# A decoder kernel: the clearing of a sorted buffer is issued later in SP's queue, from other zeros

## The reference

```python
x = x + attention(layernorm(x))          # linear attention, 16 heads, elu(q), elu(k), silu(v), gate silu(u)
x = x + experts(layernorm(x), token_ids) # 4 experts, each with one 512 x 512 matrix ctx[e] as gate, up and down
x = x + ffn(x)                           # W_up, W_gate, W_down of 2048 x 512, made ternary by their mean |w|
```

## Time and profile before

| | us |
|---|---|
| median of 3 runs | 761.21 (761.17 to 762.01) |
| the profiled execution, its own time | 762.63 |
| its span, first to last instruction | 761.0 |
| TensorE busy | 714.1 (94% of the span) |
| VectorE busy | 388.2 |
| ScalarE busy | 276.2 |
| GpSimd busy | 108.1 |
| mean granted clock of TensorE | 0.978 of full speed |

### The profile page before, as it was taken

The page is one execution under the profiler, slowest core; times in us unless marked ns, Lnnn a source line. Parts: engine busy times, 40 slices in busy tenths (PEclk is TensorE's granted clock), DMA queues, the critical chain, the costliest instruction groups (busy, mean ns, idle before and its releaser), DMA issues.

```text
span 761.0 us, 11666 instructions
## 1 busy us (share of the span) xinstructions
PE 714.1 (94%) x3804; PEld 378.2 (50%) x3835; DVE 388.2 (51%) x672; ACT 276.2 (36%) x430; POOL 108.1 (14%) x154
## 2 busy tenths in 40 slices
PE   5899999999996789999995999999999999999997
PEld 2356557557555476555544444444444444444443
DVE  5658766666645856444447444454343544343223
ACT  3355545545544264322223222222222222222221
POOL 4203025024021400000014100000000000000000
PEclk9999999999998989999998799999999999999999
DMA  7975025034035395322212111112011200020001
GB/s 213 390 277 199 1 112 166 0 118 158 1 129 203 111 344 182 126 94 85 83 41 84 28 28 28 28 46 66 14 28 28 83 20 21 14 69 1 0 0 56
DMA packets 45165, 69.88 MB, mean 92 GB/s; under 512 B 19024, under 2 KB 19024, under 8 KB 44112
## 3 DMA queue, kind: packets, MB, share of 16 engines
q1 hardware_dynamic: 41136, 56.38, 22.6%
q0 software_dynamic: 4000, 13.11, 4.9%
HBM read 47.73 MB, written 18.61 MB: 87 GB/s over the span
## 4 chain that ended last, share of the span: by engine, by line
PE 86%; DVE 4%; DMA 3%; issue 2%; ACT 2%; SPq 1%; POOL 1%; DVEq 0%; ACTq 0%; POOLq 0%
PE bank L1079 33%; PE bank L1335 29%; PE bank L1345 14%; PE bank L1072 6%; PE bank L1222 2%; PE bank L1236 1%; DMA nrm<-in_L_ffn_W_down_dram 1%; PE bank L1257 1%; DMA stage<-in_L_attn_Wv_dram 1%; DVE w_att L864 1%; SPq L184 1%; DVE w_att L863 0%; DMA n<-sorted_outputs,pos_now 0%; POOL rs L320 0%; DVE st L589 0%
## 5 line engine op out<-in xcount | busy, mean ns | idle before, releaser
L1335 PE MATMUL bank<-w_att,region 128*128 128x512 f16 (+1 forms) x1024 | 233.6, 382 | 0.9 <-ACT w_att L550 0.8
L1335 PEld LDWEIGHTS bank<-w_att,region 128*128 (+1 forms) x1024 | 100.7, 98 | 123.8 <-issue 4.8
L1045 DVE SCALAR_TENSOR_TENSOR tmp<-tmp,hk,bank 128x512 f32<-128x512 f32 x64 | 47.8, 747 | 150.8 <-PE bank L1335 150.4
L1345 PE MATMUL bank<-region,tmpA 128*128 (+1 forms) x474 | 116.8, 379 | 1.6
L1079 PE MATMUL bank<-w_moe,tmpA 128*128 x456 | 104.6, 379 | 1.5 <-DVE tmpA L934 1.5
L1079 PE MATMUL bank<-xT,w_att 128*128 128x512 f16 x384 | 89.2, 389 | 6.1 <-DVE region L774 4.4
L564 ACT ACTIVATE tmp<-bank,qs 128x512 f32<-128x512 f32 x64 | 44.0, 687 | 119.9 <-PE bank L1335 119.9
L568 ACT ACTIVATE tmpA<-tmp 128x512 f16<-128x512 f32 x64 | 40.3, 629 | 122.1 <-DVE tmp L1045 122.1
L1345 PEld LDWEIGHTS bank<-region,tmpA 128*128 128x128 f16 x504 | 49.2, 98 | 59.6 <-DVE stage L1028 0.9
L1079 PEld LDWEIGHTS bank<-w_moe,tmpA 128*128 128x128 f16 x456 | 44.4, 98 | 47.1 <-issue 1.7
L1048 DVE TENSOR_TENSOR tmpA<-tmp,tmpA 128x512 f16<-128x512 f32 x64 | 44.3, 693 | 45.6 <-ACT tmpA L568 45.6
(11 more groups left out here) (136 smaller groups left out, 746.8 us busy)
## 6 DMA issues: line engine op xcount, KB each, us to landing
stage<-in_L_ffn_W_up_dram SPq DMA_DIRECT2D x8, 1024.0 KB, 5.3
stage<-in_L_ffn_W_gate_dram SPq DMA_DIRECT2D x8, 1024.0 KB, 5.4
sorted_tokens<-a SPq DMA_DIRECT2D x10, 512.0 KB, 11.1
n<-sorted_tokens SPq DMA_DIRECT2D x20, 256.0 KB, 2.6
stage<-in_ctx_dram SPq DMA_DIRECT2D x4, 1024.0 KB, 6.6
stage<-in_L_ffn_W_down_dram SPq DMA_DIRECT2D x4, 1024.0 KB, 7.7
nrm<-in_L_ffn_W_down_dram SPq DMA_DIRECT2D x4, 1024.0 KB, 7.3
out_dram<-stage SPq DMA_DIRECT2D x16, 256.0 KB, 2.1
```

The lines of the kernel that those rows point to most:

```text
L1045: dve.scalar_tensor_tensor(out=h32, in0=sil, scalar=hk[:, 0:1], in1=gate_ps[:, :], op0=ALU.mult, op1=ALU.mult).then_inc(s["hid_mul"], 1)
L1335: mm = pe.matmul(dst, w[:, bass.ds(cf_c, 1), k * P:(k + 1) * P].rearrange("p a n -> p (a n)"), x3T[:, bass.ds(b, 1), i, k].rearrange("p a ...
L1345: mm = pe.matmul(ffy_ps[t][:, :], hid[:, parity, i, t * P:(t + 1) * P], tern[2][:, bass.ds(c, 1)].rearrange("p a n -> p (a n)"), start=(st ...
```

## The change

The stores of zeros leave `weights(0, True)` and stand behind it, so between the four loads of batch 0 and those of batch 1. Their source is no longer `a32` but `zeros`, the high part of expert 3 in `w_moe`, of the same size (128 x 1024 float32). GpSimd's memset fills that part instead. Since `a32` no longer holds the zeros, `gated_mul` waits for `zeroed` no more; ScalarE, which writes `w_moe[:, 3]`, waits for it in the last batch.

```diff
+    zeros = w_moe[:, E - 1, 0].rearrange("p k d -> p (k d)").bitcast(F32).rearrange("p (a d) -> p a d", d=D)
...
                 summed_unit(b, 0, 1)
-
-                sp.wait_ge(s["zero_src"], 1)
-                with sp.Fori(0, (SLOTS + 1) // 2) as i:
-                    sp.dma_start(xs_v[:, bass.ds(2 * i, 2)], a32[:, :, :]).then_inc(s["zeroed"], 16)
             else:
...
         weights(0, True)
+        sp.wait_ge(s["zero_src"], 1)
+        with sp.Fori(0, (SLOTS + 1) // 2) as i:
+            sp.dma_start(xs_v[:, bass.ds(2 * i, 2)], zeros).then_inc(s["zeroed"], 16)
         with sp.Fori(1, B) as b:
             weights(b, False)
...
-        pool.memset(a32[:, :, :], 0.0).then_inc(s["zero_src"], 1)
+        pool.memset(zeros, 0.0).then_inc(s["zero_src"], 1)
...
             else:
+                if last:
+                    act.wait_ge(s["zeroed"], 16 * ((SLOTS + 1) // 2))
                 ctx_hi(b, 0)
...
             if k == 0:
-                dve.wait_ge(s["zeroed"], 16 * ((SLOTS + 1) // 2))
                 dve.wait_ge(s["u_act"], K * b + K)
```

## The result

The changed kernel takes 770.78 us (median of 4 runs, 769.48 to 773.01), the kernel before 761.22 in the same comparison. The ratio is 1.0128 (95% interval 1.0105 to 1.0151): slower by 9.6 us, where 7.6 were forecast. A second comparison gave 771.17 us and 1.0121 (1.0095 to 1.0146).

What follows compares the result with a forecast made beforehand. TensorE was taken to bound the kernel, so a late load costs it the wait. 0 for the removal, 5.8 us of waiting and 1.8 us of lowered clock added 7.6 to 761.2: 768.8 us, range 765.5 to 771.5.

Steps and rivals of the forecast that it cites:

- What bounds the kernel: TensorE holds 86% of the chain; a late transfer matters only if TensorE waits, then costs nearly its full lateness.
- Removed from 26.7 us: Taking the ten stores from 26.7 us on SP's queue helps nothing that anyone waits for: gain 0.
- sign of being wrong: Instructions of the stretch 26 to 54 us starting earlier than before would show the forecast wrong.
- rival "faster": The stores had slowed compute at 26 to 52 us; a hole of 1.1 us closes, giving 760.1 us; chance 2%.
- Added at 55 us: The ten stores ahead of ctx(1) in SP's queue make it land at 78.5 us (77.1 to 79.3), not 69.94.
- rival "hidden": ctx(1) shares the engines with the zeros or is served early and lands before 72.2 us; chance 6%.
- the slowest of the 16 engines: The last DMA engine ends 1.8 us behind the bulk at ctx(1)'s landing; bounds 0.4 and 2.6.
- Who waits: TensorE's four transposes in batch 1 wait for ctx(1), delaying the products behind them by 5.8 us (4.4 to 6.6).
- The clock: After TensorE's idle the granted clock falls to 1.2 GHz for the 24 matmuls: 1.8 us lost (0 to 2.9).
- rival "only the wait, no clock": TensorE waits for ctx(1) but is granted full speed: 767.0 us; chance 10%.
- Others: up(1), down(0) and GpSimd's bias additions cost 0; changed waits on DVE and ScalarE stay under 0.1 us together.
- rival "more": A later laggard engine, or a low clock spreading to v's products, gives 770.7 up to 773 us; chance 12%.

Runs made afterwards that it cites:

- e3: Changed kernel with the ten stores moved behind the loads of ctx(1) and up(1), ahead of gate(1): 761.25 us, ratio 0.9987 to the kernel before.
- e4: Changed kernel with five of the ten stores back at the old place, five behind the loads of batch 0: 761.11 us, ratio 1.0015 to the kernel before.
- e5: Changed kernel with three stores at the old place, seven behind the loads of batch 0: 766.82 us, ratio 1.0082 to the kernel before.
- e11: Changed kernel with nine further 512 KB stores of zeros behind the ten, all ahead of ctx(1): 783.08 us, ratio 1.0294 to the kernel before.
- e7: Changed kernel with 28 unread matmuls in TensorE's wait for ctx(1), batch 1 standing ahead of its loop: 765.92 us, ratio 1.0056 to the kernel before.
- e8: As e7 with the number of unread matmuls set to 0, batch 1 still ahead of TensorE's loop: 768.96 us, ratio 1.0107 to the kernel before.
- e1: Changed kernel with the ten stores kept at the old place, between up(0) and gate(0), only the source new: 761.45 us, ratio 0.9999 to the kernel before.
- e6: Changed kernel with the ten stores issued by GpSimd on its own queue instead of by SP: 768.91 us, ratio 1.0115 to the kernel before.
- e9: Changed kernel with ctx's first quarter transposed behind q's fourth product, not the second, in batches 1 to 3: 765.61 us, ratio 1.0041 to the kernel before.

## Why the prediction was right

**What bounds the kernel.** Right. A late transfer cost TensorE its lateness, and nothing behind gave it back: +9.55 us by batch 3, and spans that differ by 9.4 (770.4 and 761.0) though this execution was 1.02 ahead at the start.

**Removed from 26.7 us: 0.** Right, by e3, and by the 43.47 us from 22.50 to 65.97, the same as before. Instructions of 26 to 54 us do start earlier, which the forecast named as a sign of being wrong. But they were ahead by the same 1.02 us before the old place of the stores, so it isn't that sign. The rival "faster" falls.

**Added at 55 us.** The mechanism is right, by the series of e4, e5, the changed kernel and e11. The rival "hidden" falls. Issuing took 12.43 us for ten stores, 12.8 expected, but the reasoning behind it was off: it took 1.28 us as the pace of stores that are not held up, and e4 issues five in 3.86 us, 0.8 each. The size of ctx(1)'s delay was short: landing 24.4 us behind gate(0)'s issue was forecast (78.5 - 54.11), and it was 25.9 (78.95 - 53.09). The terms that were mis-sized are the rate at the seam, 0.9 us as above, and the slowest of the 16 engines. The bulk through ctx(1), 8.39 MB, is reached at 76.6 us by the sum of the stretches, so the last engine is 2.3 us late, where I took 1.8. That was within the bound of 2.6. The landing itself, 79.97 in the time of the kernel before (78.95 + 1.02), lies above the bounds of 77.1 to 79.3.

**Who waits.** Right: the four transposes wait 7.68 us, and DVE's q_elu was done well before. Forecast 5.8 us, measured 7.5, above the upper bound of 6.6: 1.5 by the landing, and 0.2 because the transposes themselves ran at 1.2 GHz, which I had not counted.

**The clock.** Forecast 1.8, measured 2.0 on the products, and 2.6 for transposes and products together in the pair e7 and e8. The rival "only the wait, no clock" (767.0) falls: the 24 products took 7.38 us behind the idle, and 5.34 where e7 filled it.

**Others.** GpSimd's additions ran at 76.69, up(1) was not waited for, the moved wait on ScalarE cost nothing (e1). Right.

**The sum.** 7.6 forecast, 7.5 + 2.0 = 9.5 in the profile and 9.6 by the medians. 770.78 lies within 765.5 to 771.5, but above the single forecast and close to the upper end. That it lies within is in part luck: the wait exceeded its bound by 0.9 us, and the range held because its clock term reached up to 2.9 where 2.0 was measured. It is the rival "more" (770.7 up to 773) by its figure, through one half of that rival's reasons: the laggard engine and the seam, not a clock that stayed low for longer.

## What to carry to other kernels

A transfer that nobody waits for still stands in front of those issued behind it. So ask of each place in a queue which load comes next, when it is needed and how many bytes lie ahead of it: here 1.41 us for each 512 KB. Count the time in which the engines would have stood idle as room too: the margin at the use was 2.2 us, but some four stores would have been free (an estimate from e4 and e11). Two loads further back (e3) the same stores cost nothing. Another queue is no way round it while the same 16 engines serve both (e6). Where TensorE's wait can't be avoided, independent matmuls moved into it (e9) or even useless ones (e7) save the 2 to 2.6 us of the lowered clock.

## What had not been expected of the hardware

- At the seam from loads to stores the rate fell to 262 and 363 GB/s for 4 us (the changed kernel, 58 to 62 us). e5_split7 has 299 and 304 in 56 to 60 us, and e7_warm 321 and 297 in 58 to 62. Its cause is open.
- The step of the clock doesn't grow with the idle: 24 products took 7.43 us behind 4.05 us of idle, 7.92 behind 4.11 (e6), 7.38 behind 7.68 and 7.49 behind 20.81; behind 1.85 us of idle (e7) they took 5.34.
- A load in SP's queue got no packets for 3.4 us (e6, 62.55 to 66 us) while GpSimd's queue was served, and from 68 us on one packet for each of the other's (147 and 148 in 68 to 70 us).
